# Flamingo stack on one core: query layout copied within SBUF, new units for the side products, and the last sixteen units' expert stages in a bank of their own

## The reference, cut to what matters

```python
x = x + tanh(g_xattn[0]) * quantised_matmul(layernorm(x), ctx)
x = x + tanh(g_ffn[0]) * low_rank_fourier_ffn(layernorm(x))
# stage 3: the 128 units
q = (ln(x) @ Wq.T) ; k, v = (cat(ctx, ln(x)) @ Wk.T, ... @ Wv.T)     # 16 heads of 96, 4 KV heads
attn = softmax(q @ k.T / sqrt(96)) ; x = x + tanh(g_xattn[1]) * ((attn @ v) @ Wo.T)
# stage 4: the expert stages
flat = layernorm(x) ; scores = softmax(flat @ router_weight.T + router_bias)
topk_w, topk_idx = top_k(scores, 8)
w_dense = zeros((T, 64)).at[rows, topk_idx].add(topk_w)
x = x + tanh(g_ffn[1]) * (flat * topk_w.sum(-1) + w_dense @ expert_bias)
```

## Time and profile before

| quantity | value |
| --- | --- |
| median of three runs | 1058.85 us |
| profiled execution, its own time | 1056.73 us |
| span of the profiled execution | 1055.0 us |
| mean granted TensorE clock | 0.993 |
| stage 3, first scores to end of the last round | 332.34 to 1018.35 us |
| starts of rounds 0 to 7 | 332.34, 421.38, 506.96, 590.73, 675.42, 758.70, 843.47, 927.20 us |

### The profile page before, as it was taken

One profiled execution on the slowest core, in us unless ns is written; L12 is line 12 of the kernel. 1 busy time (PEld: TensorE's weight loads), 2 busy tenths in 40 slices (PEclk: granted clock), 3 DMA queues, 4 the chain that ended last, 5 costly groups with the idle time before them and its releaser, 6 DMA issues.

```text
span 1055.0 us, 18610 instructions
## 1 busy us (share of the span) xinstructions
PE 1005.6 (95%) x7262; PEld 554.5 (53%) x7262; DVE 640.9 (61%) x1109; ACT 655.7 (62%) x711; POOL 646.0 (61%) x348
## 2 busy tenths in 40 slices
PE   9999999999999998999999999999999999988897
PEld 4555444444544454555555555555555555555553
DVE  6889849644225365556655555655655665666767
ACT  5786535431224586666777766767766767777764
POOL 4476779242000578856767956668865667787771
PEclk9999999999999999999999999999999999999999
DMA  9886664843323999999999999999999999899995
GB/s 342 259 302 214 201 211 122 183 82 60 84 78 98 172 201 213 208 221 175 210 201 192 197 227 204 189 212 185 202 213 210 187 212 193 138 203 179 176 190 160
DMA packets 521179, 198.04 MB, mean 188 GB/s; under 512 B 485876, under 2 KB 503988, under 8 KB 521092
## 3 DMA queue, kind: packets, MB, share of 16 engines
q1 hardware_dynamic: 521092, 196.86, 90.0%
HBM read 59.24 MB, written 13.63 MB: 69 GB/s over the span
## 4 chain that ended last, share of the span: by engine, by line
PE 69%; DMA 9%; DVE 6%; ACT 5%; POOL 4%; SPq 4%; issue 3%; DVEq 0%; ACTq 0%; POOLq 0%
PE ps L588 33%; PE ps L844 10%; PE ps L804 9%; PE ps L867 8%; DMA region_o<-region_y 5%; PE ps L869 4%; DVE p_max L1634 3%; ACT p L1304 2%; POOL region_y L1799 2%; PE ps L824 2%; SPq L549 2%; PE ps L610 1%; DMA region_c<-region_b 1%; SPq L551 1%; ACT region_b L1040 1%
## 5 line engine op out<-in xcount | busy, mean ns | idle before, releaser
L1799 POOL TENSOR_TENSOR region_y<-p,region_b 128x1536 f16<-128x1536 f32 x128 | 397.1, 3103 | 268.8 <-ACT region_b L1040 241.7
L1304 ACT ACTIVATE p<-ps,p_max 128x1536 f32<-128x1536 f32 x128 | 196.8, 1537 | 131.8 <-DVE p_max L1634 131.4
L1634 DVE TENSOR_REDUCE p_max<-ps 128x1 f32<-128x1536 f32 x128 | 224.6, 1755 | 65.4 <-PE ps L824 33.3
L1040 ACT ACTIVATE region_b<-p 128x1536 f16<-128x1536 f32 x128 | 189.7, 1482 | 57.1 <-DMA region_c<-region_b 49.5
L867 PE MATMUL ps<-region_q,region_c 128*128 128x192 f16 x1536 | 208.7, 247 | 16.7 <-DMA region_o<-region_y 11.4
L869 PE MATMUL ps<-region_q,region_o 128*128 128x96 f16 x1536 | 203.3, 206 | 0.0
L844 PE MATMUL ps<-region_q,region_c 128*128 128x512 f16 x768 | 187.4, 380 | 0.0
L867 PEld LDWEIGHTS ps<-region_q,region_c 128*128 128x128 f16 x1536 | 150.6, 98 | 40.6 <-issue 20.9
L869 PEld LDWEIGHTS ps<-region_q,region_o 128*128 128x128 f16 x1536 | 150.6, 98 | 11.8 <-issue 0.6
L588 PE MATMUL ps<-region_w,region_q 128*128 128x512 f16 x576 | 138.2, 386 | 9.4 <-issue 5.8
L804 PE MATMUL ps<-ln_t,region_w 128*128 128x512 f16 x576 | 132.7, 382 | 1.9 <-issue 1.9
(11 more groups left out here) (161 smaller groups left out, 1210.2 us busy)
## 6 DMA issues: line engine op xcount, KB each, us to landing
stage<-ctx_in SPq DMA_DIRECT2D x16, 512.0 KB, 4.9
stage<-ctx_t_in SPq DMA_DIRECT2D x15, 512.0 KB, 8.7
stage<-wq_in SPq DMA_DIRECT2D x16, 384.0 KB, 4.3
stage<-wo_in SPq DMA_DIRECT2D x16, 384.0 KB, 4.4
k_scratch<-region_o SPq DMA_DIRECT2D x12, 384.0 KB, 5.9
region_q<-k_scratch SPq DMA_DIRECT2D x8, 576.0 KB, 5.5
...
```

What stands on the lines that cost most here:

```text
L1040: return nc.scalar.activation(out, in_, ACT.Copy)
L1304: nc.scalar.activation(p32[:, m % 2, :], rows, ACT.Exp, bias=p_max[:, m % 4:m % 4 + 1], accum_out=den[:, m % 4:m % 4 + 1]).then_inc(e32_ok, 1)
L1634: nc.vector.reduce_max(p_max[:, m % 4:m % 4 + 1], rows, axis=AX, negate=True).then_inc(max_ok, 1)
L1799: return nc.gpsimd.tensor_tensor(out, a, b, op)
```

## The change

- **Query layout.** From round 1 on `take_q` writes only one copy of the 512 columns from PSUM, and `double_q` makes the second one later from SBUF, behind the narrow copy of the probabilities. It is counted by `q_dup`, for which TensorE waits at the first unit of a round. Round 0 keeps the double copy.
- **Units of the side products.** `Q_AT`, `Q_AT_FIRST` and `WO_AT` have other units. Free of side products in rounds 1 to 6 are now units 0 and 12 instead of 0 and 1, in round 0 units 4, 8, 10 and 12. The splits of the output weights go from units 7 to 10 to units 8 to 11, the loads of the query weights one unit later. The first half of a query product waits for half of the weights only. The output weights of head group 0 are loaded in units 3 to 6 of round 0 instead of before unit 0, keys and values of round 1 in unit 7 instead of 4. `spread_low_q` issues one DMA in each of two units.
- **The last sixteen units.** Routers, turned weights and mixes all use bank 7, at units 3, 4, 8 and 12 (routers); turned weights and four mixes stand behind the weighing of their unit. `side_free` waits for logits, mixes and turned weights. The fifth router (index 4) runs behind the last unit, its exponential behind `expert_norm(5)`, its choice behind an output tile.

```diff
-    Q_AT = {4: (0, 0), 5: (0, 1), 8: (1, 0), 9: (1, 1), 10: (2, 0), 11: (2, 1)}
-    Q_AT_FIRST = {2: (0, None), 4: (1, 0), 5: (1, 1), 7: (2, 0), 8: (2, 1)}
+    Q_AT = {1: (0, 0), 2: (0, 1), 5: (1, 0), 6: (1, 1), 9: (2, 0), 10: (2, 1)}
+    Q_AT_FIRST = {2: (0, 0), 3: (0, 1), 5: (1, 0), 6: (1, 1), 7: (2, 0), 9: (2, 1)}
     V_AT = {0: 2, 1: 3}
-    WO_AT = {2: 4, 3: 5, 6: 6, 7: 7, 12: 0, 13: 1, 14: 2, 15: 3}
-    WO_AT_LAST = {1: 4, 2: 5, 5: 6, 6: 7, 9: 0, 10: 1, 13: 2, 14: 3}
-    WO_SPLIT, WQ_SPLIT = {7: 0, 8: 1, 9: 2, 10: 3}, {12: 0, 13: 1, 14: 2, 15: 3}
-    WQ_LOAD, WO_LOAD = {8: 0, 9: 1, 10: 2, 11: 3}, {3: 0, 4: 1, 5: 2, 6: 3}
+    WO_AT = {3: 4, 4: 5, 7: 6, 8: 7, 11: 0, 13: 1, 14: 2, 15: 3}
+    WO_AT_LAST = {1: 4, 2: 5, 5: 6, 6: 7, 9: 0, 10: 1, 14: 2, 15: 3}
+    WO_SPLIT, WQ_SPLIT = {8: 0, 9: 1, 10: 2, 11: 3}, {12: 0, 13: 1, 14: 2, 15: 3}
+    WQ_LOAD, WO_LOAD = {9: 0, 10: 1, 11: 2, 12: 3}, {3: 0, 4: 1, 5: 2, 6: 3}
     LAST = NU - UPS
     STATS4 = {-2: 0, 0: 1, 3: 2, 7: 3, 11: 4, 15: 5}
     NORM4 = {-1: 0, 1: 1, 4: 2, 8: 3, 12: 4}
     LOW4 = {0: 0, 2: 1, 5: 2, 9: 3, 13: 4}
-    ROUTE = {2: 0, 4: 1, 7: 2, 11: 3, 15: 4}
-    CHOOSE = {3: 0, 5: 1, 8: 2, 12: 3}
-    CHOOSE_REST = {4: 0, 6: 1, 9: 2, 13: 3}
-    TURN_W = {5: 0, 8: 1, 10: 2, 14: 3}
-    SCALE_X = {5: 0, 8: 1, 10: 2, 14: 3}
-    MIX = {7: (0, 0), 8: (0, 1), 11: (1, 0), 12: (1, 1), 15: (2, 0)}
-    STORE = {9: 0, 13: 1}
+    ROUTE = {3: 0, 4: 1, 8: 2, 12: 3}
+    CHOOSE = {4: 0, 5: 1, 9: 2, 13: 3}
+    CHOOSE_REST = {5: 0, 6: 1, 10: 2, 14: 3}
+    TURN_B = {5: 0, 6: 1, 10: 2, 14: 3}
+    SCALE_X = {5: 0, 6: 1, 10: 2, 14: 3}
+    MIX, MIX_B = {7: (0, 0), 11: (2, 0)}, {7: (0, 1), 8: (1, 0), 9: (1, 1), 11: (2, 1)}
+    STORE = {9: 0, 11: 1, 13: 2}
     def wo_n(g):
...
         sp.wait_ge(v4_st, 32)
-        for s in range(RING):
-            load_wo(0, s)
-
-        def spread_low_q(t):
+        def spread_low_q(t, n):
             b = t % B
             sp.wait_ge(q_free, 2 * NJ * (t + 1))
-            for n in range(2):
-                sp.dma_start(q_head[HD:P, b, 0:NJ, n, :], q_rest[b][n * HP:(n + 1) * HP, 0:NJ, :]).then_inc(q_ld[b], 16)
+            sp.dma_start(q_head[HD:P, b, 0:NJ, n, :], q_rest[b][n * HP:(n + 1) * HP, 0:NJ, :]).then_inc(q_ld[b], 16)
         def copy_last_q(t):
...
                 turn_o(o_at(m))
             if m - LAST in LOW4:
                 turn4(LOW4[m - LAST])
-            if t < TS - 1 and u == q_done(t) + 1:
-                spread_low_q(t + 1)
-            if t < TS - 1 and u == q_done(t) + 2:
+            if t < TS - 1 and u in (q_done(t) + 1, q_done(t) + 2):
+                spread_low_q(t + 1, u - q_done(t) - 1)
+            if t < TS - 1 and u == q_done(t) + 3:
                 copy_last_q(t + 1)
             if m >= PT:
                 sp.wait_ge(pv_ok, m - PT + 1)
...
                              ).then_inc(v4_st, 16)
-            if m == 4:
+            if m == 7:
...
                 load_wq(t // 2 + 1, WQ_LOAD[u])
+            if t == 0 and u in WO_LOAD:
+                load_wo(0, WO_LOAD[u])
             if t % 2 == 1 and u in WO_LOAD and t < TS - 1:
                 load_wo(t // 2 + 1, WO_LOAD[u])
             if m - LAST in STORE:
...
             elif u == 0:
                 pe.wait_ge(q_free, 2 * NJ * (t + 1))
+                pe.wait_ge(q_dup, G * t)
                 pe.wait_ge(q_ld[b], 64 * ((t + t % 2) // 2))
             if m >= 2:
...
-        def side_free(m):
+        def side_free(m, second=False):
             before = range(m)
             if 0 < m < UPS:
                 pe.wait_ge(v_lo_ok, 5 * 4 + 2 + sum(v in V_AT for v in before))
             pe.wait_ge(q_free, 2 * (NJ + sum(q_end(v) is not None for v in before)))
-            if any(wo_at(v) is not None for v in before):
-                pe.wait_ge(wo_free, sum(wo_at(v) is not None for v in before))
-            if any(v - LAST in MIX for v in before):
-                pe.wait_ge(fin_ok, sum(v - LAST in MIX for v in before))
+            outs = sum(wo_at(v) is not None for v in range(m + second))
+            if outs:
+                pe.wait_ge(wo_free, outs)
+            last = m - LAST
+            if last >= 0:
+                routed = sum(v < last + second for v in ROUTE)
+                mixed = sum(v < last + second for v in MIX) + sum(v < last for v in MIX_B)
+                turned_w = sum(v < last for v in TURN_B)
+                if routed:
+                    pe.wait_ge(lg_step, routed)
+                if mixed:
+                    pe.wait_ge(fin_ok, mixed)
+                if turned_w:
+                    pe.wait_ge(wx_ok, turned_w)
         pe.wait_ge(k_lo_ok, 6 * NJ)
         for m in range(NU):
...
                 pe.wait_ge(v_lo_ok, 5 * 4 + 2)
             scores(m)
             last = m - LAST
-            if last in ROUTE:
-                pe.wait_ge(o_ok, m - LAG)
-                router(6, ROUTE[last])
-            if last in TURN_W:
-                pe.wait_ge(o_ok, m - LAG)
-                expert_turn(6, TURN_W[last])
             w = wo_at(m)
             if m in V_AT:
                 side_free(m)
                 value_product(7, V_AT[m])
             elif q_at(m) is not None:
                 j, part = q_at(m)
+                pe.wait_ge(w_split, wq_n((t + 1) // 2) + (RING // 2 if part == 0 else RING))
                 if part != 1:
-                    pe.wait_ge(w_split, wq_n((t + 1) // 2) + RING)
                     side_free(m)
                 q_product(7, (t + 1) % B, j, part)
             elif w is not None:
                 pe.wait_ge(w_split, wo_n(w // 16) + RING // 2 * (w % 2 + 1))
                 side_free(m)
                 out_product(7, w)
+            elif last in ROUTE:
+                side_free(m)
+                router(7, ROUTE[last])
             elif last in MIX:
                 side_free(m)
                 expert_mix(7, *MIX[last])
             if m >= LAG:
-                if last in ROUTE:
-                    pe.wait_ge(lg_step, ROUTE[last] + 1)
-                if last in TURN_W:
-                    pe.wait_ge(wx_ok, TURN_W[last] + 1)
                 weigh(m - LAG)
+            if last in TURN_B:
+                side_free(m, second=True)
+                expert_turn(7, TURN_B[last])
+            elif last in MIX_B:
+                side_free(m, second=True)
+                expert_mix(7, *MIX_B[last])
...
         turn_last(0, 30, (0, 1, 2))
-        pe.wait_ge(fin_ok, 5)
-        expert_mix(7, 2, 1)
         weigh(NU - 3)
+        pe.wait_ge(fin_ok, 6)
...
         expert_turn(5, 4)
-        pe.wait_ge(fin_ok, 6)
+        pe.wait_ge(lg_step, 5)
         expert_mix(7, 3, 1)
         pe.wait_ge(wx_ok, 5)
...
             for h, rows, part in q_rows(j):
-                both = bank(at)[part, :].unsqueeze(1).broadcast_to((part.stop - part.start, 2, 512))
-                nc.scalar.activation(q_head[rows, t % B, h, :, :], both, ACT.Copy, scale=SCALE
-                                     ).then_inc(q_hi, 1)
+                if t == 0:
+                    both = bank(at)[part, :].unsqueeze(1).broadcast_to((part.stop - part.start, 2, 512))
+                    ins = nc.scalar.activation(q_head[rows, 0, h, :, :], both, ACT.Copy, scale=SCALE)
+                else:
+                    ins = nc.scalar.activation(q_head[rows, t % B, h, 0, :], bank(at)[part, :], ACT.Copy, scale=SCALE)
+                ins.then_inc(q_hi, 1)
+
+        def double_q(t, h):
+            act.wait_ge(q_hi, 2 * (NJ * t + min(h, NJ - 1)) + (2 if h == G - 1 else 1))
+            copy(q_head[0:HD, t % B, h, 1, :], q_head[0:HD, t % B, h, 0, :]).then_inc(q_dup, 1)
         def take_o(k):
...
             if o_at(m) is not None and m < NU - 1:
                 take_o(o_at(m))
-            if last in TURN_W:
-                expert_weights(6, TURN_W[last])
+            if last - 1 in TURN_B:
+                expert_weights(7, TURN_B[last - 1])
             rows = ps[:, NSB * (m % 2):NSB * (m % 2 + 1), :].rearrange("p b n -> p (b n)")
             act.wait_ge(max_ok, m + 1)
             if m >= 2:
...
                 act.wait_ge(pt_hi_ld[(m - 2) % PT], use(m - 2, PT))
             act.wait_ge(e32_ok, m + 1)
             copy(p_hi[:, m % 2, :], p32[:, m % 2, :]).then_inc(exp_ok, 1)
+            if q_end(m) is not None:
+                double_q(t + 1, q_end(m))
+            if t < TS - 1 and u == q_done(t) + 1:
+                double_q(t + 1, G - 1)
             if t % 2 == 0 and u in WO_SPLIT:
                 if t > 0:
...
         take_last(1, 0, 30, slice(0, 3))
         expert_norm(5)
+        expert_exp(4)
...
                 take_out(m - LAG)
+            if last in MIX_B:
+                add_mix(7, *MIX_B[last])
             if last in STATS4:
                 expert_stats(STATS4[last])
...
         take_low_last(1, 0, 30, slice(0, 3))
         invert(NU - 3)
         take_out(NU - 3)
-        add_mix(7, 2, 1)
+        logits(7, 4)
+        add_out(1, 60)
         choose(4, 4)
-        add_out(1, 60)
```

7 lines of the change are left out of this document (4 added, 3 removed).

## The result

The changed kernel takes 1063.45 us (median of six runs, 1062.36 to 1065.55), the one before 1058.59 in the same series. The ratio is 1.0052, its 95% interval 1.0033 to 1.0071: slower by 0.5%, 4.9 us, where I forecast 1055. The ratio is made of the fast executions alone, without the one of the kernel before that took 2085.79 us. By the bound of 2% it is no change; by its interval it is a small loss.

A forecast was written before the change was run, and what follows sets the result against it. TensorE, busy 1005.6 of 1055.0 us, was taken as the bound. Terms -7.2 - 1.6 - 5.0 + 13.5 - 2.5 + 0 + 1 = -1.8 us on the profiled 1056.73 gave 1055, 8-in-10 range 1040 to 1066.

The forecast's parts named there:

- query copies: Query products copied out of bank 7: narrower copies end the issue waits before side products, -7.2 us, range -7.7 to 0.
- rounds 1 to 6: Middle rounds: -1.6 for exponential waits, -5.0 for low-half waits, +13.5 for the new wait at unit 13 with its clock.
- not shorter: Rival on query copies: half the columns cost the same, the 7.2 us stay, SBUF copies add work; 1063 us, chance 0.06.
- The first 18 units: Start of the kernel: better spread products -6, four weight loads +3.4; taken as -2.5 us, from -6 to +4.
- The wait at unit 13: Rounds 2, 4, 6: output product 1 waits 2.9 us for GpSimd's last weight split, +8.7 us, +13.5 with slow clock.
- The clock loss: Behind each wait at unit 13: a lowered clock costs 1.6 us, three times, +4.8 us; 0 if it stays up.
- The waits for the exponential in middle rounds: Even units following a free odd unit in rounds 1 to 6: four score-bank waits of 0.4 us go, -1.6 us.
- The waits for low halves: Weighings in rounds 1 to 6 waiting for transposed low weights: of 5.2 us, -5.0 us, range -5.2 to 0.
- The last sixteen units: Last round: old waits go, up to -10 us, but new waits come at later units; 0, from -7 to +6.
- The end: Behind the last round: router 4's exponential stands behind a normalisation and VectorE's choice waits; +1 us, from 0 to 2.
- my own signs: Trace: no issue waits; even rounds wait about 3 us at unit 13; rounds near 82 and 86; last about 91 us.
- The rival that ended slower: Last round: late router exponentials delay the scores' exponentials and idle time lowers the clock; 1065 us, chance 0.14.

The follow-up runs named there:

- e6: The kernel before with the query copies alone (512 columns from PSUM, second copy inside SBUF), all units as before: 1049.4 us, ratio 0.9916.
- e7: Query copies and new side-product units as in the changed kernel, last sixteen units and end as in the kernel before: 1058.25 us, ratio 0.9997.
- e11: e7 with all round 0 units and loads as in the kernel before: 1053.5 us, ratio 0.9963.
- e2: The changed kernel with the output weights of head group 0 loaded before unit 0 again: 1059.6 us, ratio 1.0008.
- e3: The changed kernel with output product 1 at unit 14, 2 at 15, 3 at unit 0 of the next round: 1063.3 us, ratio 1.0046.
- e14: e3 with GpSimd's query weight splits and ScalarE's copies of these weights both cut to 8 columns: 1062.6 us, ratio 1.0041.
- e13: e6 with new units in odd rounds only, and the first half of a query product waiting for half the split weights: 1047.2 us, ratio 0.9894.
- e8: The kernel before with the new units, loads and splits alone, wide copies and old last round: 1070.8 us, ratio 1.0112.
- e1: The changed kernel with keys and values of round 1 loaded in unit 4 again instead of unit 7: 1062.6 us, ratio 1.0035.
- e4: The changed kernel with the fifth router's exponential ahead of the normalisation of tile 5 on ScalarE: 1059.1 us, ratio 1.0014.
- e5: The changed kernel with query products again copied from PSUM to both places by one 1024-column instruction: 1073.8 us, ratio 1.0148.
- e15: e13 with the changed kernel's last round, end and later low-query spread, fifth router's exponential ahead of the normalisation: 1052.0 us, ratio 0.9932.
- e17: e15 with the spread of the low queries as in the kernel before: 1049.4 us, ratio 0.991.

## Why the prediction was wrong

The terms, each kernel first taken against the kernel before of its own series (each term is good to about 3 us):

| term | predicted | measured | from |
| --- | --- | --- | --- |
| query copies | -7.2 | -8.8 | e6 against before |
| round 0 | -2.5 | +4.3 | e7 against e11 |
| rounds 1 to 6 | -1.6 - 5.0 + 13.5 = +6.9 | +4.5 | e11 against e6 |
| last round and end | 0 + 1 | +4.8 | changed kernel against e7 |
| sum | -1.8 | +4.9 | changed kernel against before |

- **The query copies: right.** Width sets the time, two copies save 0.85 us for 0.8, and all 7.7 us of issue waits went. The rival "not shorter" is out. That the whole came near 7.2 is in part luck: the waits for low halves grew by 5.9 us in e6, and time was gained elsewhere.
- **The first 18 units: the step that failed.** I took -2.5, from -6 to +4; what was measured, +4.3, lies at the bad end. I had weighed the loads rightly (3.4 against 3.9 us), but credited 6 us for better spread products. I had worked out the late split for "rounds 2, 4, 6" and left out round 0, which is even too and has the same table of splits; there the product at unit 13 waits longest, 3.8 us, and the one at unit 11 as well, 1.8. By e2 the loads are 3.7 to 3.9 of the 4.3 us, so all the rest of the new round 0 cost about 0.5 us where I had credited 6. In the trace TensorE idles 12.9 us in the first 18 units (101.04 less 88.17), where it idled 11.5 before; the waits for the splits, 5.6 us together, took the place of those that the spread removed. How much of them the late split alone would cost was not tried.
- **The wait at unit 13: right in place, cause and size.** 2.6 us for 2.9, three times. The clock loss was mis-sized: 1.6 for each was charged, and in the profiled execution it came once in these rounds. The 28 us of idle time that I gave GpSimd in a round are those of an odd round; in round 2 of the kernel before it is busy for 62.7 of 83.8 us.
- **The waits for the exponential in middle rounds: right.** The four of 0.4 us at unit 2 are gone.
- **The waits for low halves: failed.** I took back 5.0 of 5.2 us. In rounds 1 to 6 those of 0.3 us and more were 7.3 us before and are 7.4 after, at unit 0 above all, which is short now: 2.5, 1.2, 0.6, 0.9 and 0.3 us in rounds 1 to 5. In e3 and e14 TensorE waited for transfers at the end of an even round as soon as the wait ahead of it was gone.
- **The last sixteen units: right in the waits, within the range in size.** The two traces differ by +0.2 us for 0 in the first fifteen units, but that is one pair of executions: with the old order these units take 81.5 (e13) to 87.0 us (e8) in seven traces, with the new one 85.7 to 86.9 in the changed kernel, e1, e2, e4, e5 and e15 to e17. The waits stand where they were counted: 2.7 us at unit 4 (4.6 foreseen), 1.45 at unit 9 (1.8), 1.55 at unit 11 (2.2), 3.0 at unit 14 (3.7), each for the cause given (at unit 9 the profile names none; VectorE's rows do: the choice waited 1.5 us for the logits, which ScalarE had behind a normalisation, and the output product in bank 7 was added only behind the choice). By medians this part with its mended end is a loss of 1 to 2 us.
- **The end: mis-sized.** I named the choice that waits for an exponential behind the normalisation and priced it at 1 us, from 0 to 2. It is about 4 (4.35, or 3.9 against the own series). The normalisation and its copy do not only take 2.2 us (1026.69 to 1028.92), they wait 3.7 for GpSimd first, and I had not followed its own input.

Round 0 and the end are together about 10 us off (6.8 and 2.9 to 3.35), of which the other terms take 3 back. Another 2 of the 8.4 us between 1055 and 1063.45 are the start: I added the sum to the profiled execution, 1056.73, and not to the median.

Of my own signs these came: no issue waits before the products, one wait of 2.6 us at unit 13 of each even round, odd rounds at 82.0 and 83.1 (84.2 in round 1), even ones at 87.1, 86.0 and 83.8, the last round as long as before with its longest wait, 3.0 us, at unit 14. The clock behind the wait stayed up in two rounds of three. The sign that failed is the one of the failed step: the first 18 units at 101.0 for 95 us.

The rival that ended slower (late exponentials in the last round) is not what happened, although its time, 1065, is the nearest.

The four loads cost 3.9 us in e2. The Trainium skill, DMA: Bandwidth & Descriptors, section Latency and other measured facts, gives transposes an effective 261 GB/s (where the middle dimension is not contiguous). From it I had estimated 48 us for a round's transposes, with room for the loads. The measurement decides against that conclusion; no run here isolates the 261 GB/s themselves.
